# The second store of a recurrence's values goes to ScalarE's queue, and TensorE gets 56 spare products ahead of its first sum pair

## The reference

```python
w = jnp.exp(-jnp.exp(time_decay + jnp.tanh(xw @ decay_w1) @ decay_w2)).reshape(B, L, H, S)
r = (xr @ Wr.T).reshape(B, L, H, S)
k = (xk @ Wk.T).reshape(B, L, H, S)
v = (xv @ Wv.T).reshape(B, L, H, S)
g = jax.nn.silu(xg @ Wg.T)
def step(s, inp):
    k_l, v_l, w_l, r_l = inp
    a = k_l[..., :, None] * v_l[..., None, :]
    out = jnp.einsum('bhs,bhst->bht', r_l, faaaa * a + s)
    s_new = a + w_l[..., None] * s
    return (s_new, out)
```

## Time and profile before

| | |
|---|---|
| median of 3 runs | 913.14 us (912.07 to 915.74) |
| the profiled execution | 913.19 us, of which 911.4 us lie between the first and the last instruction |
| busy share of the span | PE 94%, DVE 62%, ACT 47%, POOL 25% |
| mean granted TensorE clock | 0.985 of full speed |

### The profile page before, as it was taken

One profiled execution on the slowest core, in us unless ns is written; L12 is line 12 of the kernel. 1 busy time (PEld: TensorE's weight loads), 2 busy tenths in 40 slices (PEclk: granted clock), 3 DMA queues, 4 the chain that ended last, 5 costly groups with the idle time before them and its releaser, 6 DMA issues.

```text
span 911.4 us, 17166 instructions
## 1 busy us (share of the span) xinstructions
PE 859.8 (94%) x6636; PEld 670.1 (74%) x6636; DVE 563.8 (62%) x1310; ACT 429.3 (47%) x965; POOL 228.7 (25%) x242
## 2 busy tenths in 40 slices
PE   6677999999999998999999999999989999999998
PEld 5656777776867765676787777877767777888987
DVE  3498999999999988552233453333334365544654
ACT  3313242424242435344666685757656785333442
POOL 3455555464646457200000000000000000110100
PEclk9988999999999998999999999999999999999999
DMA  7657655554547352104002020102140231000200
GB/s 270 156 104 224 164 144 155 145 149 141 153 117 172 96 152 74 50 21 116 8 8 85 8 63 2 62 2 62 29 184 1 104 120 77 0 0 0 82 0 35
DMA packets 44424, 80.56 MB, mean 88 GB/s; under 512 B 21485, under 2 KB 27629, under 8 KB 42558
## 3 DMA queue, kind: packets, MB, share of 16 engines
q1 hardware_dynamic: 44350, 79.55, 30.9%
HBM read 70.36 MB, written 9.18 MB: 87 GB/s over the span
## 4 chain that ended last, share of the span: by engine, by line
PE 46%; ACT 3%; DMA 1%; issue 1%; DVE 1%; SPq 0%; DVEq 0%
PE bank L1851 9%; PE bank L1838 8%; PE bank L1709 8%; PE bank L1715 7%; PE bank L1801 4%; PE bank L1793 3%; PE bank L1823 3%; PE bank L1757 2%; PE bank L1743 2%; ACT smb L1289 2%; DMA cx<-latc_scratch 1%; ACT pts L1297 1%; PE bank L1811 1%; PE bank L1464 0%; ACT cx_hi L1180 0%
## 5 line engine op out<-in xcount | busy, mean ns | idle before, releaser
L900 DVE CUSTOM_DVE_ANT_0 smb<-bank,mask 112x487 f32<-112x487 f32 x128 | 78.1, 660 | 125.8 <-issue 125.8
L693 DVE TENSOR_TENSOR_SCAN scan<-bank,scan 128x448 f32<-128x448 f32 x128 | 132.0, 1073 | 8.4 <-POOL scan L547 8.4
L1470 PEld LDWEIGHTS bank<-xj,front 128*128 128x128 f32 x1024 | 119.5, 196 | 13.6 <-issue 8.1
L544 POOL TENSOR_TENSOR scan<-scan,ks 128x896 f32<-128x896 f32 x64 | 124.2, 1940 | 10.1 <-DMA scan<-v_scratch 9.8
L1470 PE MATMUL bank<-xj,front 128*128 128x112 f32 x1024 | 121.9, 280 | 4.9 <-POOL xj L535 4.9
L1289 ACT ACTIVATE smb<-smb,nmax 112x487 f32<-112x487 f32 x128 | 88.3, 691 | 65.4 <-DVE nmax L900 64.9
L521 POOL TENSOR_TENSOR small<-small,neghalf 112x1 f32<-112x1 f32 x24 | 13.4, 560 | 367.9 <-DVE small L932 274.0
L700 DVE TENSOR_TENSOR scan<-scan,bank 128x896 f32<-128x896 f32 x64 | 68.8, 1077 | 0.8
L535 POOL TENSOR_TENSOR xj<-tmp,xa 128x448 f32<-128x448 f32 x40 | 42.5, 1064 | 81.0 <-DVE tmp L662 81.0
L1801 PE MATMUL bank<-ident,smb 112*122 112x112 f32 x512 | 56.9, 262 | 4.1 <-ACT smb L1289 3.7
L1801 PEld LDWEIGHTS bank<-ident,smb 112*122 112x122 f32 x512 | 52.3, 139 | 10.0 <-ACT smb L1289 5.8
(11 more groups left out here) (195 smaller groups left out, 1759.1 us busy)
## 6 DMA issues: line engine op xcount, KB each, us to landing
scan<-v_scratch SPq DMA_DIRECT2D x64, 448.0 KB, 5.7
cx<-in_ctxt SPq DMA_DIRECT2D x8, 750.0 KB, 5.4
raw_w<-in_wbig SPq DMA_DIRECT2D x4, 1024.0 KB, 8.0
w<-in_w SPq DMA_DIRECT2D x2, 2048.0 KB, 7.9
v_scratch<-vt SPq DMA_DIRECT2D x64, 56.0 KB, 1.8
w<-in_w SPq DMA_DIRECT2D x1, 3328.0 KB, 11.1
tail<-in_wbig SPq DMA_DIRECT2D x3, 1024.0 KB, 10.5
front<-in_wbig SPq DMA_DIRECT2D x2, 1024.0 KB, 10.0
```

The source lines that it names most:

```text
L544: g.tensor_tensor(buf[:, :, :], buf[:, :, :], ks[b % 2][:, k:k + 1, 0:T].broadcast_to([P, VS, T]), ALU.mult).then_inc(s["a_ready"], 1)
L693: n = v.tensor_tensor_scan(flat, decay, flat, 0.0, ALU.mult, ALU.add)
L900: v.tensor_tensor_reduce(sm[r], bank[r][0:T, 0:NKEY], mask_b[b % 2][:, :], -1.0 / DH, 3e38, ALU.add, ALU.min, nmax[:, h:h + 1]).then_inc(s ...
L1470: i = t_.matmul(tiles(dst)[:, m, :], w[:, k, m * P:(m + 1) * P], x[:, k, :], start=k == 0, stop=k == NT - 1)
```

## The change

`store_values` on SP keeps only the first copy (four DMAs). The second copy is issued by ACT, by a new `store_second_values`, straight behind the copy that makes `vt`. SP still waits for all eight landings before it reads. And period 0 of TensorE begins with 56 spare products.

```diff
             def store_values(d):
                 sp.wait_ge(s["vt_ready"], d + 1)
                 by_quad = v_scratch[d].rearrange("h r (j k) t -> j r h k t", j=NT, k=NT)
                 for j in range(NT):
-                    for r in range(2):
-                        sp.dma_start(by_quad[j, r], vt[j * H:(j + 1) * H, :, 0:T]).then_inc(s["v_stored"], 16)
+                    sp.dma_start(by_quad[j, 0], vt[j * H:(j + 1) * H, :, 0:T]).then_inc(s["v_stored"], 16)
                 sp.wait_ge(s["v_stored"], 32 * NT * (d + 1))
...
+            def store_second_values(d):
+                act.wait_ge(s["vt_ready"], d + 1)
+                by_quad = v_scratch[d].rearrange("h r (j k) t -> j r h k t", j=NT, k=NT)
+                for j in range(NT):
+                    act.dma_start(by_quad[j, 1], vt[j * H:(j + 1) * H, :, 0:T]).then_inc(s["v_stored"], 16)
...
                 if 0 <= i + 1 < B:
                     values(i + 1)
+                    store_second_values(i + 1)
                 if 0 <= i < B:
                     decays(i, 3)
...
                 if i == 0:
+                    spare_products(56)
                     sum_pair(0, 0)
```

## The result

The changed kernel takes 916.67 us (median of 20 runs, 909.78 to 919.98), the kernel before 912.55 (20 runs, 909.77 to 915.74): 1.0045 as a ratio of medians. The comparison's own estimate, which is the ratio given from here on, is 1.0039 with the interval 1.0026 to 1.0052. The forecast was 914.8 in a range of 911 to 921, and it called anything under 0.5% no change; what is measured lies under 0.5%, and above zero. Two more comparisons of the same two kernels are among the experiments; they gave 1.0002 (0.9985 to 1.0019) and 1.0026 (1.0008 to 1.0045). So the change costs from next to nothing to 0.4%; the plain mean of the three is 0.2%, 2 us. The profiled execution of the changed kernel has a span of 915.3 us against 911.4.

The account below looks back on a forecast made before the run. PE is busiest on the page, but the prediction took DVE to bound the first layer's periods (busy 41.22 of 42 us). Terms 0.26 + 0 + 1.32 = 1.6 us on the profiled 913.19 gave 914.8, range 911 to 921.

Parts of the forecast that it names:

- The price of an issue: On ACT, taken from SP's stores: four issues in 1.78 us, putting off work behind the values' copy by 1.9 us.
- The shared descriptor maker: Rival: SP and ACT share one descriptor maker, eight stores still take 3.72 us, time about 927; chance 0.19.
- Startup, +0.9: Before period 0: spare products delay PE by 2.7 us, full clock gives back 1.8, so 0.9 us lost.
- Period 0, +0.64 and -1.28: Last decays come 0.64 us too late for DVE's scan; DVE's wait for sequence 1's first chunk then absorbs 1.28.
- and +0.26 is left: Net loss of 0.26 us claimed after startup and period 0, once the chunk wait has absorbed 1.28.
- The sum: All terms, 0.26 + 0 + 1.32, claimed to cost 1.6 us and give 914.8 us.
- the rival of the cheap issue: ACT's issues cost about 0.1 us; DVE's 0.9 us deviation wait may go too, giving 911.0; chance 0.14.
- Periods 1 to 5, 0: Delay of 1.9 us fits the 2.16 us to spare before the scan behind the last decays: no cost.
- the cover: The 2.16 us to spare before that scan in periods 1 to 5; each period costs any excess above it.
- Period 6, +1.32: Keys had 0.58 us of idle time; the rest of 1.9 lengthens DVE's wait for ACT's columns by 1.32 us.

Follow-up runs that it names:

- e6: Changed kernel plus 9 further spare products ahead of the sum pair in period 0's second gap; 914.07 us, ratio 1.0015.
- e9: Changed kernel, last sequence's second store on SP, spare products 5 before startup mixes, 38 before first sum pair, 9 in second gap; 908.09 us, ratio 0.9951.
- e5: Changed kernel with all eight stores issued by ACT and none by SP; 934.37 us, ratio 1.0230.
- e8: Changed kernel again, unedited, second comparison with the kernel before; 914.34 us, ratio 1.0002.
- e4: Changed kernel with the last sequence's second copy stored by SP instead of ACT; 914.25 us, ratio 1.0009.
- e10: Changed kernel a third time, unedited, third comparison with the kernel before; 915.5 us, ratio 1.0026.
- e3: Changed kernel with 38 spare products instead of 56; 912.97 us, ratio 1.0003.
- e11: Kernel before, all stores on SP, with 47 spare products added ahead of the first sum pair; 913.37 us, ratio 1.0003.
- e7: Changed kernel without spare products and with the last sequence's second store on SP; 911.08 us, ratio 0.9981.
- e1: Changed kernel without the 56 spare products, so only the store has moved; 911.91 us, ratio 0.9989.
- e12: e9 with SP's 16 small norm-vector loads moved ahead, behind the block weights; 909.36 us, ratio 0.9982.

## Why the prediction was right, and where it was not

**The price of an issue: right.** ACT's four issues took 1.84 us in the startup and 1.78 to 2.03 in the seven later bursts, the work behind them was put off by 1.9, as taken from SP's own stores.

**The shared descriptor maker: refuted for issues like these.** Eight stores on two queues took the time of four (1.77 beside 1.84). The rule of the Trainium skill's page "DMA: Bandwidth & Descriptors", section Queues, rings and completion order, that SP and ACT have rings but no descriptor generator of their own, read as taking turns, would have made ACT wait for SP; no such wait is in the usual issue times. The rare long issues, which in e6 and e9 end on both queues at the same moment, are the part of it that stays open. The same page's section Issuing engines are not separate DMA queues, by which issuing on several engines saves the sequencer's time, agrees with the trace: SP's stores take 1.77 instead of 3.72 us.

**Startup, +0.9: measured +1.09** (ledger, the same in all three profiles of the change). The spare products end at 52.04 for a forecast of 52.2, with the values' copy 0.25 us earlier than in the forecast: counted from that copy they end 0.1 later. The term's two parts were of the right kind: 56 products are more than the wait, and the full clock gives most of it back.

**Period 0, +0.64 and -1.28: measured +0.80 and -1.35.** Right in both.

**The step that failed: "and +0.26 is left".** The sum had no term for PE's clock at the end of period 0; only a rival let it change there, and only to give something back. With the decays 0.8 us later PE's wait ahead of the sum pair grew from 1.19 to 1.99 us, and the clock fell before the receptance product instead of before the gate product. In the three profiles DVE lost 2.4, 1.0 and 1.0 us at L700 by this, and won back 0.9, 0.6 and 0.8 by 95.7 us, the deviation's wait, which stood only in the rival of the cheap issue. At that point the three stand at +2.1, +1.0 and +0.8, for the +0.26 of the forecast.

**Periods 1 to 5, 0: right in two of three profiles,** and e5 shows the cover's size. In e8 period 1 cost 0.5 us, since PE at half clock was late with the values. The prediction took the cover from DVE and ACT alone.

**Period 6, +1.32: measured +1.3** in all three, and 0 in e4.

**The sum.** 1.6 forecast, 0.2, 2.4 and 3.6 us measured in three comparisons (their ratios times 913). In the ledger the three profiles stand at +3.4, +2.8 and +2.1 at the columns, where the forecast's terms come to +1.6. The terms for the issues are right, and so is the sign in two of the three comparisons; the one with e8 can't be told from no change. That the number came near is in part luck: the missing term was worth 0.6 to 1.8 us.

Why the comparisons differ by more than each one's interval can be seen from the mean granted clock of each execution. In the first comparison the changed kernel took 917.7 to 920.0 us in the four executions with a mean of 0.985, and 909.8 and 910.3 in the two with 0.994; in e8 the one with 0.994 took 909.8 too. At 0.987 or less were 7 of 20 executions in the first comparison, 4 of 12 in e10 and 1 of 12 in e8, in the order of the three ratios. A line through the 20 has 0.9 us for each 0.001. As an estimate from the span of 915 us: 1.8 us at half clock lower the mean by 0.001 and cost PE 0.9 us of work. So most of the spread is time that PE ran at half clock. What makes one execution have more of it is open; the startup, the second gap and period 7 are where the profiles here differ.

## What to carry over

A filler that keeps an engine's clock up must end before the wait does that it fills: size it to the wait as it will be after all other edits, since the change that shortens the wait and the filler were here in one edit and spoiled each other. Where work is put behind DMA issues on a compute engine, price each issue, and look for the slack of what is queued behind it period by period: 2.16 us of slack made 1.9 us free, as long as PE was on time, and 4.0 us cost 1.7 to 1.9 each time. A slow clock that costs little where it falls can be moved, by an edit elsewhere, to a product that somebody waits for.

## What the runs showed of the hardware

Two queues' issues run side by side at nearly full pace: 1.77 and 1.84 us for four each in the startup, where four on one queue took 1.78. Single issues of these stores are now and then 2 to 5 times as long as the usual 0.45 us: 2.25 and 1.93 us in e9, 1.52 and 1.38 in e6, 0.92 and 1.67 in e3, 2.36 in e11 and 1.34 in the kernel before, where SP issued alone. Where one was over 1.3 us long and both queues issued, the other's was long too; in e6 and e9 the two ended at the same moment, in e3 1 us apart. Those of e9, e11 and e3 came 2 to 3 us behind 16 small loads, the others did not, and in period 0 of e6 and e8 the stores followed such loads by 0.8 and 1.6 us without a long one. That points to something that both queues share; what it is, the trace doesn't show.

The length of a wait does not decide alone whether PE's clock falls. These are the waits ahead of the second sum pair and of the gate product, and what the two products behind them took, in us (3.8 is the full clock; in e9 and e12 9 spare products stand ahead of the first wait):

| profile | wait, sum pair | receptance | wait, gate | gate |
|---|---|---|---|---|
| before | 1.19 | 3.83 | 3.58 | 6.65 |
| e11 | 1.02 | 3.83 | 3.66 | 5.57 |
| changed | 1.99 | 6.07 | 0 | 3.74 |
| e8 | 2.01 | 4.59 | 0.20 | 3.83 |
| e10 | 1.99 | 5.11 | 0.20 | 3.83 |
| e7 | 1.99 | 5.45 | 0.26 | 3.83 |
| e3 | 2.45 | 5.45 | 0.75 | 3.83 |
| e1 | 1.99 | 3.83 | 2.47 | 5.45 |
| e9 | 0.73 | 3.83 | 1.69 | 5.45 |
| e12 | 0.54 | 3.83 | 1.66 | 3.83 |

With the same wait of 1.99, e1 kept the clock through the first product and e7 lost it there. Behind waits of 1.69 and 1.66 ahead of the gate product, e9 lost it and e12 kept it. In all of these but e12 one of the two products pays, 0.8 to 2.8 us. A slow receptance product delays the gate product's turn, so that it finds its input ready. In e1, e6 and e9 a gate product of 5.4 us left DVE no wait for the deviation at all.
